# Keys of the first cross attention: when the sums are copied, where the heads' steps stand, which engine makes the low parts, and the order of the loads

## The chip, the core and the metric

The kernel runs on one core of one Trainium2 chip. The metric is the device time of one execution in microseconds, from before the first to after the last instruction. A core has five engines that take their instructions in the order written, each from its own queue, and wait for each other through semaphores: TensorE (PE, matmuls), VectorE (DVE), ScalarE (ACT), GpSimd (POOL) and SyncE (SP, which here only issues DMAs).

## The reference, cut to what matters

The whole is a decoder of two layers, each with a state-space block, a cross attention and a mixture of experts. The change touches the keys' half of the first cross attention, which has no softmax, so that keys and values can be multiplied first:

```python
# B = 4 batches, S = 1601 rows of context, D = 256, 16 heads of 64 (1024 columns)
c = layernorm(context) * ln1_g + ln1_b          # [B, 1601, 256]
K = l2norm_per_head(c @ wk)                     # [B, 1601, 16, 64]
V = c @ wv
attended = l2norm(Q) @ (K^T V) @ wo             # per head; K^T V = (K^T c) wv
```

The kernel computes G = c^T K (256 x 1024, summed over the 1601 rows of a batch), then for each pair of heads (128 columns) wv^T G, of which it keeps the two 64 x 64 blocks on the diagonal, and multiplies these with wo into P[b], which the queries' stage uses.

## The kernel before, in words

**Tiles.** 1601 rows are 13 tiles of up to 128 rows (`ST` = 13, the last has 65); with 4 batches there are 52 tiles, counted by i, tile t = i % 13 of batch b = i // 13. Every engine runs a loop over i, of two iterations more than tiles, and its instructions stand in the order in which the loop issues them.

**One iteration on each engine.**
- PE (`keys_pe`): `k_rows(i)`, 12 matmuls of 512 columns for the keys of tile i (each product is three, since both operands are split into a high and a low part; `mm3`, L109 to L111), then `turn(i + 1)` (L116, transposes the normalized context), one head step, `g_tile(i - 2)` (12 matmuls that add to the four banks of G; it waits for the high and low parts of keys and context), and one more head step.
- ACT (`keys_act`): copy of the keys from PSUM (L1100), high parts of the turned and the plain context of tile i+1 (L1070, L1073), square (L1109), high part of the normed keys of tile i-1 (L1080), square root of the sums (L1113), a step of `keys_normed_act` (the deviation of the context's rows, which waits for the statistics; in batch 3 `q_normed_act`), and two head steps.
- DVE (`keys_dve`): low parts of the context of tile i+1 (L952 from PSUM, L954 as the difference of two SBUF tiles), sum of squares (L984), low part of the keys of tile i-1 (`low`, L960), clamp, reciprocal, product with the keys in place (L988, L990, L993, "unit"), a step of `keys_normed_dve`, which normalizes the context of the next batch (three tiles of statistics, L882 and L886, or two tiles of affine steps, L897 and L900). Batch 0 has its own context normalized in three chunks beside the first tiles, and the next batch's behind them. At t = 12 what is left of it is run at once. In batch 3 the steps are `q_normed_dve`.
- POOL: two memsets. SP: all loads at the start, and stores of zeros to two DRAM buffers.

**The end of a batch.** In iteration i = 13 b + 14 PE runs the last `g_tile` of batch b. Behind it ACT copies half of G to `gT` (L1125) and DVE the other half (L1006), each at the end of its iteration. The head steps of the batch, 16 of them, are a generator (`keys_heads_pe`, `keys_heads_act`), two steps per iteration. Odd steps: PE multiplies `gT` with `wv` (L773, signal `hv`), ACT copies two blocks to `mT` (L1045, L1046, signal `hm`). Even steps: PE waits for `hm` and multiplies `mT` with `wo` (L780), ACT copies the product to `P` (L1050). The first step stands at the end of the iteration in which `gT` is copied, so an odd step always comes behind `g_tile` and an even one ahead of it. The heads and `turn` share two PSUM banks in the order of use (`Banks`).

**Memory.** `wk` is loaded into the buffer of `gT`; ACT casts its high part (L1083) and DVE subtracts (L964, 2048 columns).

Of the kernel before, what the change touches and what calls it, by code (L numbers as in the profile page):

```python
# [19 lines left out]
ST = 13  # L20
# [132 lines left out]
def step(g):  # L153
    next(g, None)
# [513 lines left out]
def keys_make(k, ctx, m):  # L668

    al = lambda shape, name, dt=F32: k.make(shape, dt, name=name, ctx=ctx)  # L670
    m.wk = [al([128, 2, 1024], "wk", F32R)[:, :, :] for _ in range(2)]
    m.wv = al([128, 2, 1024], "wv")
    m.wo = al([128, 8, D], "wo")

    m.cx = [k.gate.XF[:, 0:ST, :], al([128, ST, D], "cx")[:, :, :]]
    m.vnT = [[al([128, 2, 128], "vnT", F32R) for _ in range(2)] for _ in range(2)]
    m.cs = [[al([128, D], "cs", F32R) for _ in range(2)] for _ in range(4)]
    m.ks = [[al([128, 1024], "ks", F32R) for _ in range(2)] for _ in range(2)]
    m.cst, m.cmv = al([128, ST, 6], "cst"), al([128, ST, 2], "cmv")
    m.csd, m.crs = al([128, ST], "csd"), al([128, ST], "crs")  # L680
    m.gT = al([128, 2, 1024], "gT")
    m.mT = al([128, 8, 128], "mT")
    m.kv = k.psum[:, 4:6, :]
    m.tb = [k.psum[:, 6, :], k.psum[:, 7, :]]
    c = m.count
    tiles = B * ST
    m.w_v = c("wv_wo", 2, 16)
    m.w_k = c("wk", 1, 16)
    m.wk_hi, m.wk_lo = c("wk_high", 1), c("wk_low", 1)
    m.mt_zero = c("mT_zeroed", 1)  # L690
    m.ctx_in = [c(f"context{i}", 4, 16) for i in range(2)]
# [12 lines left out]


def xattn0_make(k, ctx, inner):
# [10 lines left out]
    c = m.count  # L717
    m.zeros = c("zeros", 1)
    m.w_q = c("wq", 1, 16)
    m.vecs = c("rows_of_all", 6, 16)  # L720
    m.q_mv, m.q_sd, m.q_rs = c("q_mean_var", B), c("q_dev", B), c("q_inv_dev", B)
    with ExitStack() as own:
        keys_make(k, own, m)
# [88 lines left out]
def keys_pe(k, m, pe):  # L812
# [43 lines left out]
    for i in range(n_tiles + 2):  # L856
# [16 lines left out]
def keys_normed_dve(k, m, dve, b, o):  # L873
# [1 line left out]
    g1, b1 = m.vec["ln1_g"], m.vec["ln1_b"]  # L875
    dve.memset(m.cmv[:, :, :], 1.0).then_inc(*k.v.up)
    filled = k.v.last()
    dve.wait_ge(*m.ctx_in[b % 2](2 * (b // 2) + 1))
    for n, (c0, c1) in enumerate(keys_chunks(b)):
        for t in range(c0, c1):  # L880
            q = ROWS[t]
            dve.bn_stats(m.cst[0:q, t, :], cx[0:q, t, :]).then_inc(*k.v.up)  # L882
# [54 lines left out]
def keys_dve(k, m, dve):  # L937
# [15 lines left out]
        dve.wait_ge(*m.ch(i))  # L953
        dve.tensor_tensor(cl[0:q, :], m.cx[b % 2][0:q, t, :], ch[0:q, :], ALU.subtract).then_inc(*m.cl.up)  # L954

    def low(i):
        w = ROWS[i % ST]
        kh, kl = m.ks[i % 2]
        dve.wait_ge(*m.kh(i))
        dve.tensor_tensor(kl[0:w, :], m.kn[i % 2][0:w, :], kh[0:w, :], ALU.subtract).then_inc(*m.kl.up)  # L960

    dve.wait_ge(*m.w_k(0))
    dve.wait_ge(*m.wk_hi(0))
    dve.tensor_tensor(m.wk[1], m.gT[:, :, :], m.wk[0], ALU.subtract).then_inc(*m.wk_lo.up)  # L964
    dve.wait_ge(*m.vecs(5))
    ahead = keys_normed_dve(k, m, dve, 0, seen[0])
    turned(0, ahead)
    first = ahead
    for i in range(n_tiles + 2):
        b, t = i // ST, i % ST  # L970
        if i < n_tiles:
# [6 lines left out]
                    pass  # L978
            if i + 1 < n_tiles:
                turned(i + 1, ahead)  # L980
            r = ROWS[t]
            kn, sq, rn = m.kn[i % 2], m.sq[i % 2], m.rn[i % 2]
            dve.wait_ge(*m.k_sq(i))
            dve.tensor_reduce(rn[0:r, :], sq[0:r, :].rearrange("p (h j) -> p h j", h=16), AX, ALU.add).then_inc(*m.k_sum.up)  # L984
            if i:
                low(i - 1)
            dve.wait_ge(*m.k_dev(i))
            dve.tensor_scalar(rn[0:r, :], rn[0:r, :], 1e-12, None, ALU.max).then_inc(*k.v.up)  # L988
            dve.wait_ge(*k.v.last())
# [2 lines left out]
            unit = kn[0:r, :].rearrange("p (h j) -> p h j", h=16)  # L992
            dve.tensor_tensor(unit, unit, rn[0:r, :].unsqueeze(2).to_broadcast([r, 16, 64]), ALU.mult).then_inc(*m.k_unit.up)  # L993
            step(ahead)
        elif i == n_tiles:
            low(i - 1)
        step(other)
        if i >= 2 and (i - 2) % ST == ST - 1:
            for _ in other:
                pass  # L1000
            other = keys_heads_order(own)
            pb = (i - 2) // ST
            dve.wait_ge(*m.g(i - 2))
# [50 lines left out]
def keys_act(k, m, act):  # L1054
# [20 lines left out]
    def high(i):  # L1075
# [12 lines left out]
    for i in range(n_tiles + 2):  # L1088
        b, t = i // ST, i % ST
        if i < n_tiles:  # L1090
# [18 lines left out]
            act.activation(sq[0:r, :], kn[0:r, :], ACT.Square).then_inc(*m.k_sq.up)  # L1109
            if i:  # L1110
                high(i - 1)
            act.wait_ge(*m.k_sum(i))
            act.activation(rn[0:r, :], rn[0:r, :], ACT.Sqrt).then_inc(*m.k_dev.up)  # L1113
            step(ahead)
        elif i == n_tiles:
            high(i - 1)
        step(other)
        if i >= 2 and (i - 2) % ST == ST - 1:
            pb = (i - 2) // ST
            for _ in other:  # L1120
                pass
            act.wait_ge(*m.g(i - 2))
            if pb:
                act.wait_ge(*m.hv(8 * pb - 1))
            act.copy(m.gT[:, 0, :].rearrange("p (a n) -> p a n", a=2), k.psum[:, 0:2, :]).then_inc(*m.g0.up)  # L1125
            other = keys_heads_act(k, m, act, pb, own)
        step(other)
    for _ in other:
        pass
# [2 lines left out]
def keys_sp(k, m, sp):  # L1132
    d = k.d

    def context(b):
        i = b % 2
        if b >= 2:

            sp.wait_ge(*m.cl(ST * (b - 1) - 1))
            sp.wait_ge(*m.vl(ST * (b - 1) - 1))  # L1140
        sp.dma_start(m.cx[i][:, 0:12, :], d["ctx"][b, 0:1536, :].rearrange("(t p) c -> p t c", p=128)).then_inc(*m.ctx_in[i].up)
        sp.dma_start(m.cx[i][0:ROWS[12], 12, :], d["ctx"][b, 1536:S, :]).then_inc(*m.ctx_in[i].up)

    sp.dma_start(m.wq[:, :, :], d["x0wq"]).then_inc(*m.w_q.up)
    for n in ("ln1_g", "ln1_b", "ln2_g", "ln2_b", "bo", "b2"):
        sp.dma_start(m.vec[n][:, :], row_of(k, "x0" + n, D)).then_inc(*m.vecs.up)
    sp.dma_start(m.wv[:, :, :], d["x0wv"]).then_inc(*m.w_v.up)
    sp.dma_start(m.wo[:, :, :], d["x0wo"]).then_inc(*m.w_v.up)
    sp.dma_start(m.gT[:, :, :], d["x0wk"]).then_inc(*m.w_k.up)
    context(0)  # L1150
    context(1)
    sp.wait_ge(*m.zeros(0))
    for j in range(TRASH // 256):
        sp.dma_start(k.DR["m0buf"][256 * j:256 * j + 256, :].rearrange("(t p) c -> p t c", p=128), k.zt[:, :, :]) \
# [2470 lines left out]
```

## Time and profile before

| | |
|---|---|
| time, median of 3 runs | 3018.78 us (3003.39 to 3024.97) |
| profiled execution | 3017.55 us, span 3015.7 us |
| PE busy | 2438.6 us, 81% of the span |
| DVE busy | 2197.7 us, 73% |
| ACT busy | 1444.9 us, 48% |
| POOL busy | 890.4 us, 30% |
| mean granted TensorE clock | 0.896 of full speed |

The profile is of one execution; its times are from the span's start. Busy shares are means over stages with different limits. The stage of the change lies between 552 and about 1003 us. "PEclk" is the granted clock as a share of full speed.

### The profile page before, as it was taken

How to read it: one execution, taken by the hardware profiler on the slowest of the kernel's cores; microseconds unless marked ns; L12 is line 12 of the kernel's file. 1: busy time of each engine (PE TensorE's matmuls, PEld its weight loads, DVE VectorE, ACT ScalarE, POOL GpSimd, SP SyncE). 2: the span in 40 equal slices, each digit the busy share in tenths (PEclk: the TensorE clock that was granted, in tenths of full speed). 3: DMA queues.
4: the chain of work that ended last, by engine and by line, in shares of the span. 5: the costliest groups of instructions: out<-in, count | busy, mean ns of one | idle time of the engine just before them, and what ended most of it. 6: DMA issues, size and time to landing. Idle time of an engine off the chain costs nothing.

```text
span 3015.7 us, 31540 instructions
## 1 busy us (share of the span) xinstructions
PE 2438.6 (81%) x10888; PEld 1591.5 (53%) x10888; DVE 2197.7 (73%) x3181; ACT 1444.9 (48%) x2547; POOL 890.4 (30%) x616
## 2 busy tenths in 40 slices
PE   4989886488888899948994598888667878799997
PEld 1333432266776565737883233343233434789997
DVE  5999999597886464326886699999955643567775
ACT  5656564245555222214563665656402435356673
POOL 2878776000000000020002377777601224100004
PEclk8999999798999799968996799999987876889999
DMA  4032030650000000022331302303056241246652
GB/s 165 2 112 99 14 113 0 242 172 1 23 1 1 33 1 1 1 103 95 106 120 42 135 24 89 112 1 113 0 130 133 48 88 51 90 144 219 222 183 84
DMA packets 100050, 249.56 MB, mean 83 GB/s; under 512 B 9410, under 2 KB 63567, under 8 KB 91944
## 3 DMA queue, kind: packets, MB, share of 16 engines
q1 hardware_dynamic: 83524, 222.64, 22.7%
q0 software_dynamic: 4608, 12.59, 1.3%
q10 hardware_dynamic: 11760, 12.32, 1.3%
q8 instruction: 87, 1.43, 0.2%
q14 instruction: 71, 0.58, 0.1%
HBM read 194.42 MB, written 53.10 MB: 82 GB/s over the span
## 4 chain that ended last, share of the span: by engine, by line
PE 46%; DVE 29%; ACT 11%; issue 9%; DMA 3%; POOL 1%; ACTq 1%; SPq 1%; another core or an unknown queue 0%; DVEq 0%; POOLq 0%
DVE psum L635 10%; PE psum L432 7%; PE psum L109 5%; PE psum L111 5%; PE psum L110 5%; PE psum L397 3%; PE psum L116 3%; DVE ch L643 3%; ACT g L3221 2%; PE psum L1238 2%; PE psum L1252 2%; ACT WH L3074 2%; PE psum L1222 2%; PE psum L1200 1%; PE psum L2523 1%
## 5 line engine op out<-in xcount | busy, mean ns | idle before, releaser
L317 POOL TENSOR_TENSOR bu<-u,row 128x1024 f32<-128x1024 f32 x254 | 597.8, 2358 | 286.7 <-DVE psum L635 190.3
L432 PE MATMUL psum<-ch,ident 128*128 128x512 f32 x1024 | 511.8, 629 | 139.6 <-DVE ch L643 139.1
L635 DVE TENSOR_TENSOR_SCAN psum<-psum,bu 128x1024 f32<-128x1024 f32 x256 | 585.4, 2287 | 18.7 <-ACT psum L514 18.5
L432 PEld LDWEIGHTS psum<-ch,ident 128*128 128x128 f32 x1024 | 188.3, 196 | 427.5 <-DVE ch L643 244.0
L514 ACT ACTIVATE psum<-dt,A 128x511 f32<-128x511 f32 x512 | 332.4, 682 | 0.4
L643 DVE TENSOR_TENSOR ch<-psum,row 128x1024 f32<-128x1024 f32 x256 | 313.0, 1223 | 7.6
L1508 POOL IOTA i<- 128x128 f32 x1 | 0.3, 346 | 758.5 <-DVEq L3366 758.5
L397 PE MATMUL psum<-hT,inw 128*128 128x512 f32 x256 | 138.8, 674 | 44.3 <-ACT sz L474 27.3
L3221 ACT ACTIVATE g<-psum,bias 128x256 f32<-128x256 f32 x248 | 101.0, 471 | 144.2 <-PE psum L111 132.3
L109 PE MATMUL psum<-WH,hs 128*128 128x256 f32 x496 | 145.7, 294 | 10.5 <-DVE hs L3301 7.1
L109 PE MATMUL psum<-xT,WH 128*128 128x256 f32 x496 | 141.2, 285 | 7.6 <-DVE xT L3264 7.6
L2651 DVE TENSOR_REDUCE mp<-psum 128x1 f32<-128x128 f32 (+1 forms) x192 | 85.7, 506 | 77.6 <-PE psum L2425 77.4
L111 PE MATMUL psum<-xT,WH 128*128 128x256 f32 x496 | 140.6, 284 | 1.1 <-issue 1.1
L110 PE MATMUL psum<-WH,hs 128*128 128x256 f32 x496 | 140.7, 284 | 0.3 <-issue 0.3
L110 PE MATMUL psum<-xT,WH 128*128 128x256 f32 x496 | 140.4, 283 | 0.6 <-DVE hs L3301 0.6
L111 PE MATMUL psum<-WH,hs 128*128 128x256 f32 x496 | 140.9, 284 | 0.0
L3301 DVE TENSOR_TENSOR hs<-g,hs 128x512 fp32r<-128x512 f32 x124 | 85.7, 692 | 73.2 <-ACT hs L3228 71.1
L2818 POOL TENSOR_SCALAR_AFFINE_SELECT pT<-pT 128x256 f32<-128x256 f32 x128 | 52.8, 414 | 265.1 <-ACT pT L2598 264.0
L3043 POOL DMA_INDIRECT R<-m1res,gi x26 | 26.7, 1025 | 344.7 <-DMA m1res<-ob 321.2
L2598 ACT ACTIVATE pT<-psum 128x1024 f32<-128x1024 f32 (+3 forms) x128 | 87.1, 706 | 85.1 <-PE psum L2508 84.2
L511 ACT COPY psum<-zero 128x2 f32<-128x2 f32 x256 | 41.2, 161 | 176.4 <-DVE ch L643 175.5
L3082 DVE TENSOR_TENSOR WH<-W,WH 128x1024 fp32r<-128x1024 f32 x96 | 113.1, 1220 | 7.9 <-ACT WH L3074 7.9
(403 smaller groups left out, 5915.1 us busy)
## 6 DMA issues: line engine op xcount, KB each, us to landing
W<-in_m1W SPq DMA_DIRECT2D x24, 2052.0 KB, 8.5
row<-Ascr SPq DMA_DIRECT2D x64, 512.0 KB, 4.8
row<-Bscr SPq DMA_DIRECT2D x64, 512.0 KB, 4.8
m1buf<-zt SPq DMA_DIRECT2D x8, 2048.0 KB, 16.8
W<-in_m0W SPq DMA_DIRECT2D x16, 1024.0 KB, 8.7
WH<-x1scr SPq DMA_DIRECT2D x16, 384.0 KB, 8.3
x1scr<-hi SPq DMA_DIRECT2D x48, 128.0 KB, 2.4
qk<-x1scr SPq DMA_DIRECT2D x16, 384.0 KB
```

What stands on the lines that cost most here:

```text
L109: pe.matmul(o, al, bh, start=start, stop=False)
L110: pe.matmul(o, ah, bl, start=False, stop=False)
L111: return pe.matmul(o, ah, bh, start=False, stop=stop)
L116: return pe.transpose(o, i, k.ident[0:n, 0:n])
L317: e.tensor_tensor(m.bu[i % 3][:, :, :], u, m.row[:, g, 0, :, :], ALU.mult).then_inc(*m.fed.up)
L397: p = pe.matmul(bank, m.inw[:, f, 128 * ob:128 * ob + 128], m.hT[:, f, :], start=f == 0, stop=f == 1)
L432: p = pe.matmul(m.y, k.ident, m.ch[i % RING_C][:, j, :], start=False, stop=g == UNITS - 1 and j == 1)
L514: e = act.activation(a[:, j, 1:T], m.dt[:, s % SIX, 1:T], ACT.Exp, scale=m.A[:, n:n + 1])
L635: dve.tensor_tensor_scan(flat, flat, m.bu[i % 3][:, :, :].rearrange("p a n -> p (a n)"), 0.0, ALU.mult, ALU.add).then_inc(*m.scan.up)
L643: dve.tensor_tensor(m.ch[i % RING_C][:, :, :], a, m.row[:, g, 1, :, :], ALU.mult).then_inc(*m.out.up)
L3082: dve.tensor_tensor(lo, w, hi, ALU.subtract).then_inc(*m.Wl.up)
L3221: e = act.activation(g[:, 256 * o:256 * o + 256], m.hb[j][:, 256 * o:256 * o + 256], ACT.Gelu_apprx_tanh, bias=m.bias[w % 3][:, 2 * j + o: ...
```

## The change

- `gT`: ACT and DVE copy G in iteration i = 13 b + 14 ahead of the square root and of the sum of squares of that iteration (`drawn`), no longer at its end.
- Heads: the new generator of head steps is made in the same iteration, but `continue` skips the step behind it, on PE, ACT and DVE. The first head step so comes in the next iteration, ahead of `g_tile`.
- Low parts of the keys and of `wk`: from DVE to POOL.
- Loads: `wk` first, then the first three tiles of context (a semaphore of their own), the two rows of the first layernorm, the rest of the context; `wq` and the other four rows come behind `wv`, `wo` and the second batch's context. DVE waits for the pieces where it uses them.

```diff
@@ -688,7 +688,7 @@
     m.w_k = c("wk", 1, 16)
     m.wk_hi, m.wk_lo = c("wk_high", 1), c("wk_low", 1)
     m.mt_zero = c("mT_zeroed", 1)
-    m.ctx_in = [c(f"context{i}", 4, 16) for i in range(2)]
+    m.ctx_first, m.ctx_in = c("context_first", 1, 16), [c(f"context{i}", 4, 16) for i in range(2)]
     m.c_mv, m.c_sd = c("context_mean_var", B + 2), c("context_dev", B + 2)
     m.c_n = c("context_normed", tiles)
     m.c_T = c("context_turned", tiles)
@@ -717,7 +717,7 @@
     c = m.count
     m.zeros = c("zeros", 1)
     m.w_q = c("wq", 1, 16)
-    m.vecs = c("rows_of_all", 6, 16)
+    m.vecs, m.ln_in = c("rows_of_all", 4, 16), c("first_ln_rows", 2, 16)
     m.q_mv, m.q_sd, m.q_rs = c("q_mean_var", B), c("q_dev", B), c("q_inv_dev", B)
     with ExitStack() as own:
         keys_make(k, own, m)
@@ -865,6 +865,7 @@
                 for _ in other:
                     pass
                 other = keys_heads_pe(k, m, pe, (i - 2) // ST, own)
+                continue
         step(other)
     for _ in other:
         pass
@@ -875,8 +876,11 @@
     g1, b1 = m.vec["ln1_g"], m.vec["ln1_b"]
     dve.memset(m.cmv[:, :, :], 1.0).then_inc(*k.v.up)
     filled = k.v.last()
-    dve.wait_ge(*m.ctx_in[b % 2](2 * (b // 2) + 1))
     for n, (c0, c1) in enumerate(keys_chunks(b)):
+        if b == 0 and n == 0:
+            dve.wait_ge(*m.ctx_first(0))
+        elif b or n == 1:
+            dve.wait_ge(*m.ctx_in[b % 2](2 * (b // 2) + 1))
         for t in range(c0, c1):
             q = ROWS[t]
             dve.bn_stats(m.cst[0:q, t, :], cx[0:q, t, :]).then_inc(*k.v.up)
@@ -890,6 +894,8 @@
                 yield
         yield
         dve.wait_ge(*m.c_sd(keys_chunk_at(b, n)))
+        if b == 0 and n == 0:
+            dve.wait_ge(*m.ln_in(1))
         dve.reciprocal(m.crs[:, c0:c1], m.csd[:, c0:c1]).then_inc(*k.v.up)
         for t in range(c0, c1):
             q = ROWS[t]
@@ -953,16 +959,15 @@
         dve.wait_ge(*m.ch(i))
         dve.tensor_tensor(cl[0:q, :], m.cx[b % 2][0:q, t, :], ch[0:q, :], ALU.subtract).then_inc(*m.cl.up)
 
-    def low(i):
-        w = ROWS[i % ST]
-        kh, kl = m.ks[i % 2]
-        dve.wait_ge(*m.kh(i))
-        dve.tensor_tensor(kl[0:w, :], m.kn[i % 2][0:w, :], kh[0:w, :], ALU.subtract).then_inc(*m.kl.up)
-
-    dve.wait_ge(*m.w_k(0))
-    dve.wait_ge(*m.wk_hi(0))
-    dve.tensor_tensor(m.wk[1], m.gT[:, :, :], m.wk[0], ALU.subtract).then_inc(*m.wk_lo.up)
-    dve.wait_ge(*m.vecs(5))
+    def drawn(i):
+
+        if i >= 0 and i % ST == ST - 1:
+            pb = i // ST
+            dve.wait_ge(*m.g(i))
+            if pb:
+                dve.wait_ge(*m.hv(8 * pb - 1))
+            dve.tensor_copy(m.gT[:, 1, :].rearrange("p (a n) -> p a n", a=2), k.psum[:, 2:4, :]).then_inc(*m.g1.up)
+
     ahead = keys_normed_dve(k, m, dve, 0, seen[0])
     turned(0, ahead)
     first = ahead
@@ -978,12 +983,11 @@
                     pass
             if i + 1 < n_tiles:
                 turned(i + 1, ahead)
+            drawn(i - 2)
             r = ROWS[t]
             kn, sq, rn = m.kn[i % 2], m.sq[i % 2], m.rn[i % 2]
             dve.wait_ge(*m.k_sq(i))
             dve.tensor_reduce(rn[0:r, :], sq[0:r, :].rearrange("p (h j) -> p h j", h=16), AX, ALU.add).then_inc(*m.k_sum.up)
-            if i:
-                low(i - 1)
             dve.wait_ge(*m.k_dev(i))
             dve.tensor_scalar(rn[0:r, :], rn[0:r, :], 1e-12, None, ALU.max).then_inc(*k.v.up)
             dve.wait_ge(*k.v.last())
@@ -992,19 +996,16 @@
             unit = kn[0:r, :].rearrange("p (h j) -> p h j", h=16)
             dve.tensor_tensor(unit, unit, rn[0:r, :].unsqueeze(2).to_broadcast([r, 16, 64]), ALU.mult).then_inc(*m.k_unit.up)
             step(ahead)
-        elif i == n_tiles:
-            low(i - 1)
+        else:
+            drawn(i - 2)
         step(other)
         if i >= 2 and (i - 2) % ST == ST - 1:
             for _ in other:
                 pass
             other = keys_heads_order(own)
-            pb = (i - 2) // ST
-            dve.wait_ge(*m.g(i - 2))
-            if pb:
-                dve.wait_ge(*m.hv(8 * pb - 1))
-            dve.tensor_copy(m.gT[:, 1, :].rearrange("p (a n) -> p a n", a=2), k.psum[:, 2:4, :]).then_inc(*m.g1.up)
+            continue
         step(other)
+    dve.wait_ge(*m.vecs(3))
 
 
 def both(a, b):
@@ -1078,6 +1079,14 @@
             act.wait_ge(*m.g(i - 2))
         act.wait_ge(*m.k_unit(i))
         act.copy(m.ks[i % 2][0][0:w, :], m.kn[i % 2][0:w, :]).then_inc(*m.kh.up)
+
+    def drawn(i):
+        if i >= 0 and i % ST == ST - 1:
+            pb = i // ST
+            act.wait_ge(*m.g(i))
+            if pb:
+                act.wait_ge(*m.hv(8 * pb - 1))
+            act.copy(m.gT[:, 0, :].rearrange("p (a n) -> p a n", a=2), k.psum[:, 0:2, :]).then_inc(*m.g0.up)
 
     act.wait_ge(*m.w_k(0))
     act.copy(m.wk[0], m.gT[:, :, :]).then_inc(*m.wk_hi.up)
@@ -1109,21 +1118,20 @@
             act.activation(sq[0:r, :], kn[0:r, :], ACT.Square).then_inc(*m.k_sq.up)
             if i:
                 high(i - 1)
+            drawn(i - 2)
             act.wait_ge(*m.k_sum(i))
             act.activation(rn[0:r, :], rn[0:r, :], ACT.Sqrt).then_inc(*m.k_dev.up)
             step(ahead)
-        elif i == n_tiles:
-            high(i - 1)
+        else:
+            if i == n_tiles:
+                high(i - 1)
+            drawn(i - 2)
         step(other)
         if i >= 2 and (i - 2) % ST == ST - 1:
-            pb = (i - 2) // ST
             for _ in other:
                 pass
-            act.wait_ge(*m.g(i - 2))
-            if pb:
-                act.wait_ge(*m.hv(8 * pb - 1))
-            act.copy(m.gT[:, 0, :].rearrange("p (a n) -> p a n", a=2), k.psum[:, 0:2, :]).then_inc(*m.g0.up)
-            other = keys_heads_act(k, m, act, pb, own)
+            other = keys_heads_act(k, m, act, (i - 2) // ST, own)
+            continue
         step(other)
     for _ in other:
         pass
@@ -1132,23 +1140,26 @@
 def keys_sp(k, m, sp):
     d = k.d
 
-    def context(b):
+    def context(b, t0=0):
         i = b % 2
         if b >= 2:
 
             sp.wait_ge(*m.cl(ST * (b - 1) - 1))
             sp.wait_ge(*m.vl(ST * (b - 1) - 1))
-        sp.dma_start(m.cx[i][:, 0:12, :], d["ctx"][b, 0:1536, :].rearrange("(t p) c -> p t c", p=128)).then_inc(*m.ctx_in[i].up)
+        sp.dma_start(m.cx[i][:, t0:12, :], d["ctx"][b, 128 * t0:1536, :].rearrange("(t p) c -> p t c", p=128)).then_inc(*m.ctx_in[i].up)
         sp.dma_start(m.cx[i][0:ROWS[12], 12, :], d["ctx"][b, 1536:S, :]).then_inc(*m.ctx_in[i].up)
 
-    sp.dma_start(m.wq[:, :, :], d["x0wq"]).then_inc(*m.w_q.up)
-    for n in ("ln1_g", "ln1_b", "ln2_g", "ln2_b", "bo", "b2"):
-        sp.dma_start(m.vec[n][:, :], row_of(k, "x0" + n, D)).then_inc(*m.vecs.up)
+    sp.dma_start(m.gT[:, :, :], d["x0wk"]).then_inc(*m.w_k.up)
+    sp.dma_start(m.cx[0][:, 0:3, :], d["ctx"][0, 0:384, :].rearrange("(t p) c -> p t c", p=128)).then_inc(*m.ctx_first.up)
+    for n in ("ln1_g", "ln1_b"):
+        sp.dma_start(m.vec[n][:, :], row_of(k, "x0" + n, D)).then_inc(*m.ln_in.up)
+    context(0, 3)
     sp.dma_start(m.wv[:, :, :], d["x0wv"]).then_inc(*m.w_v.up)
     sp.dma_start(m.wo[:, :, :], d["x0wo"]).then_inc(*m.w_v.up)
-    sp.dma_start(m.gT[:, :, :], d["x0wk"]).then_inc(*m.w_k.up)
-    context(0)
     context(1)
+    sp.dma_start(m.wq[:, :, :], d["x0wq"]).then_inc(*m.w_q.up)
+    for n in ("ln2_g", "ln2_b", "bo", "b2"):
+        sp.dma_start(m.vec[n][:, :], row_of(k, "x0" + n, D)).then_inc(*m.vecs.up)
     sp.wait_ge(*m.zeros(0))
     for j in range(TRASH // 256):
         sp.dma_start(k.DR["m0buf"][256 * j:256 * j + 256, :].rearrange("(t p) c -> p t c", p=128), k.zt[:, :, :]) \
@@ -1164,7 +1175,17 @@
 
 def keys_pool(k, m, pool):
     pool.memset(k.zt[:, :, :], 0.0).then_inc(*m.zeros.up)
+    pool.wait_ge(*m.w_k(0))
+    pool.wait_ge(*m.wk_hi(0))
+    pool.tensor_tensor(m.wk[1], m.gT[:, :, :], m.wk[0], ALU.subtract).then_inc(*m.wk_lo.up)
     pool.memset(m.mT[:, :, :], 0.0).then_inc(*m.mt_zero.up)
+    for i in range(B * ST):
+        w = ROWS[i % ST]
+        kh, kl = m.ks[i % 2]
+        if i >= 2:
+            pool.wait_ge(*m.g(i - 2))
+        pool.wait_ge(*m.kh(i))
+        pool.tensor_tensor(kl[0:w, :], m.kn[i % 2][0:w, :], kh[0:w, :], ALU.subtract).then_inc(*m.kl.up)
```

## Rows read from the trace of the kernel before

**Rows 1.** Windows: span, busy time and count of each engine, PEclk, DMA share, GB/s.

```profile
703.00:707.00 4.00, 4.00 (x12) 3.32 (x13) 0.00 (x0) 0.41 (x2) 0.00 (x0) 0.50 0.02 4
...
780.00:873.00 93.00, 84.41 (x391) 68.17 (x388) 78.93 (x147) 53.94 (x104) 0.00 (x0) 0.94 0.00 1
```

**Rows 2.** Timeline of one tile with heads: start us, us, engine, line, operation.

```profile
801.38 1.01 ACT L1100 COPY kn<-psum 128x1024 f32<-128x1024 f32 x1 [3.73 <-PE psum L111]
...
801.64 0.58 PE L109 MATMUL psum<-ks,cs 128*128 128x512 f32 x1
...
803.82 1.05 ACT L1080 CAST ks<-kn 128x1024 fp32r<-128x1024 f32 x1
...
803.96 1.22 DVE L984 TENSOR_REDUCE rn<-sq 128x16 f32<-128x1024 f32 x1 [0.51 <-ACT sq L1109]
...
804.59 0.60 PE L773 MATMUL psum<-gT,wv 128*128 128x128 f32 x4
804.95 0.48 PE L109 MATMUL psum<-wk,vnT 128*128 128x512 f32 x1
805.10 1.22 DVE L960 TENSOR_TENSOR ks<-kn,ks 128x1024 fp32r<-128x1024 f32 x1
805.22 0.21 ACT L1113 ACTIVATE rn<-rn 128x16 f32<-128x16 f32 x1 [0.35 <-DVE rn L984]
...
805.34 0.35 ACT L1050 COPY P<-psum 128x256 f32<-128x256 f32 x1
...
805.81 0.21 ACT L1046 COPY mT<-psum 64x64 f32<-64x64 f32 x1
...
806.72 1.23 DVE L993 TENSOR_TENSOR kn<-kn,rn 128x1024 f32<-128x1024 f32 x1
...
807.97 1.01 ACT L1100 COPY kn<-psum 128x1024 f32<-128x1024 f32 x1 [1.95 <-PE psum L111]
```

**Rows 3.** Timeline, from tile 14 to tile 23.

```profile
693.03 1.01 ACT L1100 COPY kn<-psum 128x1024 f32<-128x1024 f32 x1 [1.89 <-PE psum L111]
...
702.78 1.20 PE L773 MATMUL psum<-gT,wv 128*128 128x128 f32 x4 [6.81 <-DVE gT L1006]
...
708.66 1.01 ACT L1100 COPY kn<-psum 128x1024 f32<-128x1024 f32 x1 [4.23 <-PE psum L111]
...
762.58 1.02 ACT L1100 COPY kn<-psum 128x1024 f32<-128x1024 f32 x1 [1.83 <-PE psum L111]
```

**Rows 4.** Three lines of code: duration ns min/median/max, first and last start.

```profile
L317 POOL TENSOR_TENSOR bu<-u,row x254: 2335/2357/2384, 56.4 to 2181.4; 128x1024 f32<-128x1024 f32 x127
...
L150 DVE TENSOR_SCALAR xn<-X,xmv,rms x16: 389/402/2441, 11.1 to 324.7; 128x256 f32<-128x256 f32 x16
...
L2172 DVE TENSOR_TENSOR pick<-i,oo x8: 191/192/441, 2407.1 to 2598.0; 128x32 f32<-128x32 f32 x8
```

**Rows 5.** Timeline of the routing in the last stage, POOL and DVE.

```profile
2408.49 0.41 POOL L2818 TENSOR_SCALAR_AFFINE_SELECT pT<-pT 128x256 f32<-128x256 f32 x1 [4.91 <-ACT pT L2598]
2408.49 0.44 DVE L2172 TENSOR_TENSOR pick<-i,oo 128x32 f32<-128x32 f32 x1
```

**Rows 6.** DMA issues from 545 to 640 us: KB each, median us to landing.

```profile
wq<-in_x0wq SPq DMA_DIRECT2D x1, 1024.0 KB, 4.6
```

**Rows 7.** Timeline of the stage's start.

```profile
568.72 1.90 ACT L1083 CAST wk<-gT 128x2048 fp32r<-128x2048 f32 x1 [17.01 <-DMA gT<-in_x0wk]
...
575.70 0.48 DVE L897 SCALAR_TENSOR_TENSOR XF<-XF,cmv,bc 128x256 f32<-128x256 f32 x1
...
578.52 0.77 PE L109 MATMUL psum<-wk,vnT 128*128 128x512 f32 x1 [1.01 <-DVE vnT L952]
```

**Rows 8.** Timeline of batch 3, ACT.

```profile
900.59 1.01 ACT L1100 COPY kn<-psum 128x1024 f32<-128x1024 f32 x1 [1.97 <-PE psum L111]
...
908.79 0.30 ACT L1033 ACTIVATE sd<-mv,t 128x4 f32<-128x4 f32 x1 [4.14 <-DVE mv L927]
...
956.97 1.02 ACT L1100 COPY kn<-psum 128x1024 f32<-128x1024 f32 x1 [1.82 <-PE psum L111]
```

## The prediction

> **What bounds the kernel now.** I read the busy shares first (no engine is full over the whole kernel), then the windows of the key stage, 552 to 1003 us, and last its timeline tile by tile. In [rows 1] the batch from 780 to 873 us shows TensorE busy for 84.4 of 93 us with VectorE at 78.9: TensorE sets the pace and waits only in places. I measure a tile from one start of ACT's copy of the keys (L1100) to the next and call the start K; the i-th tile's is K(i). In a tile with a head step K moves by 6.59 us [rows 2], 801.38 to 807.97. TensorE has no hole in it: one head matmul pair, the 12 matmuls of `g_tile` from 801.64, the next pair at 804.59, the 12 of `k_rows` from 804.95, whose end starts the copy 3.02 us later. Less the two head pairs (0.26 from 801.38 to 801.64, 0.36 from 804.59 to 804.95) that is 5.97; each pair also breaks the stream of matmuls, and I take 5.75 for a tile without heads. So an operation taken off VectorE is worth something only where VectorE is late, above all in batch 0, where it normalizes two batches (VectorE is busy for 78.9 of 93 us in a batch in which it does one).
>
> The places where TensorE does wait are the start (first keys at 578.52 [rows 7]) and the change of batch: K(14) to K(15) takes 693.03 to 708.66, 15.6 us, with TensorE idle for 6.81 until VectorE has copied its half of the sums [rows 3]. Behind that idle the granted clock is 0.50, the 1.2 GHz level [rows 1]. From the head pair to the next copy then takes 5.88 us (702.78 to 708.66) where it takes 3.38 at the full clock (804.59 to 807.97), so an idle of several us costs about 2 us more; I take 2.0 for the part that the new order keeps.
>
> **The start.** `wq`, the first load, lands 4.6 us after its issue [rows 6]; `wk` in its place lands at 552.0 + 4.6 = 556.6. ACT's cast takes 1.9 [rows 7], to 558.6. The low part, 2048 columns, is now GpSimd's. A GpSimd TENSOR_TENSOR of 1024 columns takes 2.357 [rows 4], so 2048 take about 4.8, to 563.4. The first three context tiles (384 KB) land about 1.5 us behind `wk`, VectorE's statistics end near 560, and its affine steps (575.70 before) would start there, but they read two SBUF operands. They wait for GpSimd, as the next part shows, to 563.4. From that step to the first key matmul takes 2.8 (575.70 to 578.52): 566.2 instead of 578.5, **−12**. Without that wait it would be −15.
>
> **The port.** GpSimd and VectorE stand in each other's way in this trace: a VectorE TENSOR_TENSOR of 32 columns with two SBUF inputs takes 0.192 (median) and 0.441 when a GpSimd operation of 0.41 starts in the same moment [rows 4, 5]; a VectorE TENSOR_SCALAR of 0.402 takes up to 2.441, which is longer by 2.04 and so most of a GpSimd TENSOR_TENSOR [rows 4]. VectorE's operations with a PSUM input and one SBUF input show nothing of that. The Trainium skill, SBUF — State Buffer, section "SBUF: two separate sides", calls it an exclusive lock: whichever of the two starts first has the shared pair for its whole instruction. That is a rule against this change; by it the sum is the one that I give, and if it did not hold the sum would be that of the second rival.
>
> In a tile the low part of tile i−1 now starts at K+3.5 (the cast of 803.82 ends at 804.87 [rows 2]) and ends at K+5.9. VectorE's reduce (803.96) is over at K+3.7; its clamp of the norms and its product (`unit`, two SBUF inputs) come next. Before, the low part of 1.22 stood between them and `unit` ended at K+6.5 (806.72 + 1.14 to the next start). Now they wait for GpSimd to K+5.9, and `unit` starts 0.5 later and ends at K+7.5. So the 1.14 us taken off VectorE come back as a wait of 2.2, and VectorE is later by 1 us in a tile. Where nothing is queued behind `unit` this is hidden. For batch 0, where each tile has up to 1.9 us of normalization behind it (four affine steps of 0.48 [rows 7]), I walked the order: the second tile loses the 1.1 whole, the later ones lie between no loss (the short difference `cs` gets in ahead of GpSimd) and 0.9 each (it does not). That is −3 (a little of the gain stays) to +12 for the batch; I take **+5**, nearest to half of the tiles losing. At tile 12 VectorE drains the normalization of batch 1, 26 affine steps in a row, and GpSimd's low part now cuts in: **+2.4** (0 if it is starved instead, since that tile's `g_tile` is not due). The few other tiles without heads get 0.1 to 0.3 each: **+2**. The last low part is on the path to the last sums: 2.36 for 1.22, **+1**.
>
> **The copies of the sums and the order of the heads.** ACT and VectorE now copy at K(14)+3.0, where `g_tile` of the last tile ends, before the reduce of tile 14; TensorE meanwhile runs the keys of tile 15. K(14) to K(15) falls from 15.6 to 5.75. What is queued behind VectorE's wait is its reduce, so everything of tile 14 there is 1.6 later: `unit` ends at 7.5 and three statistics at 9.1 after K(14).
>
> What is late next is TensorE's wait for `hm`. Before, the first head step stood behind `g_tile` and the parity was: product with `wo` (L780) ahead of `g_tile`, product with `wv` (L773) behind it. ACT made `mT` at the end of the tile (805.81) and TensorE needed it only after the next keys. Now the first step stands ahead of `g_tile`. So L773 comes ahead and L780 behind `g_tile`, in the same tile, and L780 waits for the two copies to `mT`, which stand in ACT's queue behind its cast and its Sqrt. Queued behind that wait are the keys of the next tile. The Sqrt starts at K+3.84 (805.22), and with no copy to `P` ahead of them the two mT copies end at K+4.4 (5.34 to 5.81 now holds P and one of them, and each takes 0.22). L780 and its step to the next matmul take about 0.4, the keys 3.02: K+7.8. A head tile so takes 7.8 for 6.6, with TensorE idle for 1.2 from K+3.3.
>
> For tiles 14 to 23, before 762.58 − 693.03 = 69.6 [rows 3]:
> - K(14) to K(15): 5.75.
> - K(15) to K(16): VectorE's `turned(16)` is late (9.1 after K(14)), so is the reduce, and with it Sqrt and mT: 9.1 if `cs` gets in ahead of GpSimd, 12 if not, each plus up to 2 for the clock after an idle of over 2 us. I take 12.
> - Tile 17: ACT's heads wait behind its wait for the statistics `c_mv`. The like of it in batch 3 starts at 908.79, 8.2 after 900.59 [rows 8]: `unit` ends at K+6.5, so the statistics of four tiles take 1.7 behind it. Here it is one tile's, about 0.6, so 7.1, plus 1.0 for the later `unit` = 8.1. Then 0.3 for ACT's step, 0.45 for mT, 0.4 for L780, 3.02 and 2.0 for the clock: 14.3.
> - Six more at 7.8: 46.8.
>
> The sum is 78.9, **+9.3**; twice (batches 1 and 2): **+18.6**.
>
> In batch 3 ACT waits for the statistics of the queries in tiles 42, 44 and 46. The wait ends at K+8.2 and now 1.0 later, at 9.2; ACT's step 0.2, mT 0.45, L780 0.4, keys 3.02 and 2.0 for the clock make 15.2 each. K(42) to K(49) was 956.97 − 900.59 = 56.4 [rows 8] and becomes 3 × 15.2 + 4 × 7.8 = 76.8, +20.4. K(40) to K(42) was 15.6 + 6.6 by the pattern of [rows 3]; now the copy of tile 41 waits behind ACT's wait for the query statistics (`g_tile` 3.0, VectorE's copy 1.2, reduce 1.1, Sqrt, clamp and port 1.0, `unit` 1.1, statistics 1.7, ACT 0.3: 9.4, taken as 9.5), and tile 41 takes 9.8 with a cold clock: 19.3, −2.9. Together **+17.5**.
>
> The loads moved back (`wq`, four rows) are wanted some 400 us later, and SP waits for nothing new ahead of them: 0. The added waits for `context_first` and `first_ln_rows` are in the start above.
>
> **Sum**: −12 + 5 + 2.4 + 18.6 + 17.5 + 2 + 1 = +34.5. The profiled execution took 3017.55 (span 3015.7), 1.2 under the median of 3018.78, so the same difference stands on the median: **3053**.
>
> **Rivals.**
> 1. *The heads cost nothing.* If mT were ready when `g_tile` ends and the port did not bite: start −15, batch 0 −6, three changes of batch at −9.8, rest 0: −50, 2969. For it: mT is short and ACT is busy for only 58% of a batch. Against: the Sqrt at K+3.84 waits for VectorE's reduce in every tile, and `g_tile` ends at K+3.3. Chance 0.08.
> 2. *The head order costs, the port does not.* Start −15, batch 0 −6, changes and head tiles +6, +6 and +12, tail +1: +4, 3023. The decider is whether `unit` and the affine steps wait for GpSimd; against it stands [rows 5], for it that the row is of a short operation. Chance 0.22.
> 3. *Slower still by the clock*: if each hole of 1.2 us in the 24 head tiles lets the granted clock fall as the long ones do, 24 × 2 = +48 on the forecast, 3100. It decides from the point where the holes make the clock fall; rows of before show none so short and regular. Chance 0.10.
> 4. *The early start does not come* (`wk` shares the DMA engines with the loads behind it and lands as late as before): the forecast without −12, 3065. Chance 0.08.
>
> The forecast itself has 0.52; its own bounds are −3/+12 for batch 0, 9.1/14 for tiles 15, 28 and 0 to 2.5 for each cold restart (eight of them): 3025 to 3073. The range leaves out rivals 1 and 3: 3015 to 3078. One per cent, 30 us, is about what this measurement can tell from no change; that bound is at 3049. Of the forecast's 0.52 I put 0.31 above it; with rivals 3 and 4 slower is 0.49. Rival 2 and the rest of the forecast: same 0.43. Faster 0.08.
>
> **What would show it.** In the changed profile: first key matmul near 566; VectorE's `unit` with durations above 1.23 or an idle ahead of it, while GpSimd's low part runs; TensorE idle about 1.2 us ahead of L780 in each head tile, released by ACT mT, and K to K 7.8; 15.6 us gone at the changes of batch; some 5 us of idle in tiles 17, 30, 42, 44, 46. Wrong would be: no idle ahead of L780 (rival 1), `unit` ending at K+5.8 (rival 2), a granted clock of 0.50 through the head tiles (rival 3).

## The result, and the profile after

The changed kernel took 3054.02 us (median of 4 runs, 3048.01 to 3057.87) where the kernel before took 3016.77 in the same comparison: a ratio of 1.0131, 95% interval 1.0107 to 1.0155. The prediction was 3053, with a range of 3015 to 3078.

The profiled execution took 3057.87 us (span 3055.4). The same view of one tile with heads as in [rows 2], now of the changed kernel (L1109 is the copy of the keys, L1081 the cast, L990 the reduce, L1188 the low part on POOL, L1123 the Sqrt, L992 the clamp, L1046 and L1047 the copies to `mT`, L997 `unit`):

```profile
751.62 1.02 ACT L1109 COPY kn<-psum 128x1024 f32<-128x1024 f32 x1 [2.36 <-PE psum L111]
751.64 0.61 PE L773 MATMUL psum<-gT,wv 128*128 128x128 f32 x4
...
754.07 1.05 ACT L1081 CAST ks<-kn 128x1024 fp32r<-128x1024 f32 x1
...
754.21 1.22 DVE L990 TENSOR_REDUCE rn<-sq 128x16 f32<-128x1024 f32 x1 [0.47 <-ACT sq L1118]
...
755.25 2.36 POOL L1188 TENSOR_TENSOR ks<-kn,ks 128x1024 fp32r<-128x1024 f32 x1 [5.60 <-ACT ks L1081]
755.47 0.22 ACT L1123 ACTIVATE rn<-rn 128x16 f32<-128x16 f32 x1 [0.35 <-DVE rn L990]
755.59 0.19 ACT L1046 COPY mT<-psum 64x64 f32<-64x64 f32 x1
755.71 1.93 DVE L992 TENSOR_SCALAR rn<-rn 128x16 f32<-128x16 f32 x1 [0.28 <-ACT rn L1123]
755.79 0.21 ACT L1047 COPY mT<-psum 64x64 f32<-64x64 f32 x1
...
756.14 0.67 PE L780 MATMUL psum<-wo,mT 128*128 128x256 f32 x2 [1.12 <-ACT mT L1047]
...
756.46 0.59 PE L109 MATMUL psum<-wk,vnT 128*128 128x512 f32 x1
...
757.97 1.23 DVE L997 TENSOR_TENSOR kn<-kn,rn 128x1024 f32<-128x1024 f32 x1
...
759.62 1.01 ACT L1109 COPY kn<-psum 128x1024 f32<-128x1024 f32 x1 [2.40 <-PE psum L111]
```

TensorE stands idle for 1.12 us ahead of L780, released by ACT's copy to `mT`, and a tile takes 8.00. The other thing to see is the clamp: 16 columns in 1.93 us, from its start until 757.64, just behind the end of POOL's instruction at 757.61. In the view of single lines, over all 52 tiles (min/median/max in ns, as in [rows 4]; the first row is the clamp of the kernel before, L988):

```profile
L988 DVE TENSOR_SCALAR rn<-rn x52: 161/168/175, 587.1 to 972.8; 128x16 f32<-128x16 f32 x48, 65x16 f32<-65x16 f32 x4
...
L992 DVE TENSOR_SCALAR rn<-rn x52: 172/1935/1973, 578.9 to 1018.7; 128x16 f32<-128x16 f32 x48, 65x16 f32<-65x16 f32 x4
...
L997 DVE TENSOR_TENSOR kn<-kn,rn x52: 1220/1224/1226, 579.4 to 1020.9; 128x1024 f32<-128x1024 f32 x48, 65x1024 f32<-65x1024 f32 x4
...
L960 DVE TENSOR_TENSOR cs<-XF,cs x26: 410/415/2625, 570.0 to 887.5; 128x256 fp32r<-128x256 f32 x24, 65x256 fp32r<-65x256 f32 x2
```

The change of batch, as in [rows 3] (L1089 and L969 are the early copies of the sums). The 15.6 us are gone, and the next tile is the late one, with 2.11 us of idle ahead of its L780:

```profile
696.63 1.01 ACT L1109 COPY kn<-psum 128x1024 f32<-128x1024 f32 x1 [2.04 <-POOL ks L1188]
...
700.00 1.02 ACT L1089 COPY gT<-psum 128x1024 f32<-128x1024 f32 x1
...
700.30 1.22 DVE L969 COPY gT<-psum 128x1024 f32<-128x1024 f32 x1
...
703.22 1.02 ACT L1109 COPY kn<-psum 128x1024 f32<-128x1024 f32 x1 [0.33 <-PE psum L111]
...
708.73 0.67 PE L780 MATMUL psum<-wo,mT 128*128 128x256 f32 x2 [2.11 <-ACT mT L1047]
...
713.78 1.01 ACT L1109 COPY kn<-psum 128x1024 f32<-128x1024 f32 x1 [3.98 <-PE psum L111]
```

Tile 42, as in [rows 8], with the wait for the queries' statistics (L1034) ahead of `mT`; below it the windows behind, at a granted clock of 0.50:

```profile
922.66 1.01 ACT L1109 COPY kn<-psum 128x1024 f32<-128x1024 f32 x1 [4.03 <-PE psum L111]
...
931.83 0.30 ACT L1034 ACTIVATE sd<-mv,t 128x4 f32<-128x4 f32 x1 [5.12 <-DVE mv L933]
...
932.58 1.19 PE L780 MATMUL psum<-wo,mT 128*128 128x256 f32 x2 [6.54 <-ACT mT L1047]
...
938.90 1.01 ACT L1109 COPY kn<-psum 128x1024 f32<-128x1024 f32 x1 [4.72 <-PE psum L111]
```

```profile
932.00:934.50 2.50, 1.92 (x5) 1.58 (x6) 0.18 (x1) 0.80 (x4) 0.00 (x0) 0.50 0.02 7
934.50:938.50 4.00, 4.00 (x11) 3.12 (x10) 0.00 (x0) 0.00 (x0) 0.00 (x0) 0.50 0.00 0
```

The start of the stage, as in [rows 7] (L1092 is the cast of `wk`, L1180 its low part on GpSimd, L903 the first affine step); its first load is now issued at 556.12 (552.00 before):

```profile
561.03 1.90 ACT L1092 CAST wk<-gT 128x2048 fp32r<-128x2048 f32 x1 [5.21 <-DMA gT<-in_x0wk]
...
563.08 4.54 POOL L1180 TENSOR_TENSOR wk<-gT,wk 128x2048 fp32r<-128x2048 f32 x1 [6.40 <-ACT wk L1092]
...
565.69 0.18 DVE L899 RECIPROCAL crs<-csd 128x3 f32<-128x3 f32 x1 [1.82 <-DMA bc<-in_bc]
565.90 2.00 DVE L903 SCALAR_TENSOR_TENSOR XF<-XF,cmv,bc 128x256 f32<-128x256 f32 x1
```

**The stage in parts.** The starts of all 52 copies of the keys, K(0) to K(51), were read from the timeline of ACT in each run (e1 to e8 are the experiments below); the stage runs from SP's first load in it to SP's first load in the next (1003.86 before). In us of one profiled execution each:

| part | before | after | e1 | e2 | e3 | e4 | e5 | e6 | e7 | e8 |
|---|---|---|---|---|---|---|---|---|---|---|
| first load to K(0) | 31.0 | 18.7 | 19.6 | 18.6 | 18.5 | 18.6 | 19.6 | 31.3 | 18.6 | 17.9 |
| K(0) to K(12) | 82.3 | 91.7 | 89.9 | 91.6 | 82.3 | 82.2 | 85.3 | 89.9 | 82.2 | 82.5 |
| K(12) to K(13) | 21.8 | 24.1 | 23.8 | 24.0 | 21.8 | 21.8 | 23.9 | 23.7 | 21.8 | 20.7 |
| K(14) to K(15) | 15.6 | 6.6 | 6.6 | 10.2 | 6.6 | 6.6 | 6.1 | 16.7 | 6.6 | 6.6 |
| K(14) to K(23) | 69.6 | 79.0 | 63.9 | 67.2 | 76.6 | 61.1 | 76.2 | 73.7 | 59.8 | 59.8 |
| K(27) to K(36) | 69.3 | 77.4 | 63.9 | 67.2 | 76.4 | 61.2 | 77.8 | 72.4 | 59.8 | 59.9 |
| K(40) to K(42) | 21.9 | 19.7 | 15.6 | 16.8 | 20.6 | 14.9 | 19.7 | 22.8 | 15.0 | 14.9 |
| K(42) to K(49) | 56.4 | 80.3 | 60.1 | 62.2 | 75.5 | 57.9 | 77.5 | 63.3 | 50.0 | 50.0 |
| stage | 451.9 | 495.9 | 441.4 | 455.8 | 470.0 | 418.2 | 483.7 | 482.8 | 407.2 | 405.2 |

The stage is 44.1 us longer, the medians differ by 37.3. The rest is the other stages, whose code the change leaves as it is: in these two profiles the stage starts 4.1 us later (556.12 for 552.00), and the part behind it took 2011.8 us before and 2003.4 after (span less end of stage). That part lies between 2002 and 2016 in the runs e1 to e4, so a difference of a few us in the whole time says nothing of this stage, and the stage's own parts are what to read.

### The profile page after: what moved, and what is told of

It reads as the page before. It is cut to its first block, busy times and chain, and to the rows that moved or that the text cites. A ratio compares the mean times of both kernels' runs of the same rounds, so it can differ in the third digit from the quotient of the medians.

```text
span 3055.4 us, 31592 instructions
## 1 busy us (share of the span) xinstructions
PE 2444.2 (80%) x10888; PEld 1589.1 (52%) x10888; DVE 2221.6 (73%) x3128; ACT 1445.8 (47%) x2547; POOL 1017.4 (33%) x669
## 4 chain that ended last, share of the span: by engine, by line
PE 41%; DVE 29%; ACT 13%; issue 9%; POOL 3%; DMA 3%; ACTq 1%; another core or an unknown queue 0%; SPq 0%; POOLq 0%; DVEq 0%
DVE psum L635 10%; PE psum L432 6%; PE psum L109 4%; PE psum L111 4%; PE psum L110 4%; PE psum L397 3%; PE psum L116 3%; DVE ch L643 3%; ACT WH L3095 2%; ACT g L3242 2%; PE psum L1259 2%; PE psum L1273 2%; DVE rn L990 2%; PE psum L1243 2%; PE psum L1221 1%
## 5 line engine op out<-in xcount | busy, mean ns | idle before, releaser
L635 DVE TENSOR_TENSOR_SCAN psum<-psum,bu 128x1024 f32<-128x1024 f32 x256 | 585.5, 2287 | 18.8 <-ACT psum L514 18.6
L1188 POOL TENSOR_TENSOR ks<-kn,ks 128x1024 fp32r<-128x1024 f32 (+1 forms) x52 | 124.1, 2387 | 333.1 <-ACT ks L1081 333.1
```

The costliest lines, as they stand in the source:

```text
L635: dve.tensor_tensor_scan(flat, flat, m.bu[i % 3][:, :, :].rearrange("p a n -> p (a n)"), 0.0, ALU.mult, ALU.add).then_inc(*m.scan.up)
L1188: pool.tensor_tensor(kl[0:w, :], m.kn[i % 2][0:w, :], kh[0:w, :], ALU.subtract).then_inc(*m.kl.up)
```

## The experiments

Runs e1 to e3 take out one suspect each, e4 two, e6 puts one part alone into the kernel before, e5 tests the port that VectorE and GpSimd share, e7 and e8 go on from e4. Each ratio is to the kernel before, timed in the same comparison: 3014.54 us for e1 to e4, 3006.76 for e5 to e8. Between these two groups compare ratios, not times. The code shown is in extracts; `...` marks what lies between.

**e1: the order of the heads.** On PE, ACT and VectorE, with an empty step ahead:

```diff
+def one_step_later(g):
+    yield
+    yield from g
...
-                other = keys_heads_pe(k, m, pe, (i - 2) // ST, own)
+                other = one_step_later(keys_heads_pe(k, m, pe, (i - 2) // ST, own))
```

> The changed kernel, but the head steps start one step later still, so that the product with wv stands behind the tile's matmuls for the sums and the product with wo ahead of them, as before the change. Theory A (TensorE's wait for mT in each head tile, behind the matmuls for the sums, costs 1.2 to 1.4 us a tile, and 6 to 7 more where ACT waits for statistics): head tiles fall from 7.98 to about 6.6, tile 17 from 13.9 to 9, tiles 42, 44, 46 from 16.1 to 10; two batches at -15, the last at -20: about -50, 3004 us, ratio to the kernel before 0.996. Theory B (the shared port is what makes the changed kernel slow, the order of the heads is harmless): no change, 3054, ratio 1.012.

Measured: 3004.99 us, ratio 0.9969 (0.9952 to 0.9987). The batches go from 79.0 to 63.9 and from 77.4 to 63.9, K(42) to K(49) from 80.3 to 60.1, the stage from 495.9 to 441.4. That is 54.5 us off the stage for the "about 50" of theory A, and 3005 for its 3004; theory B falls. A tile (L1114 is the copy of the keys) takes 6.6, TensorE has no idle ahead of L780, and L780 uses the `mT` of the tile before:

```profile
741.49 1.02 ACT L1114 COPY kn<-psum 128x1024 f32<-128x1024 f32 x1 [1.25 <-PE psum L111]
741.51 0.60 PE L780 MATMUL psum<-wo,mT 128*128 128x256 f32 x2
...
744.69 0.63 PE L773 MATMUL psum<-gT,wv 128*128 128x128 f32 x4
...
746.64 0.21 ACT L1052 COPY mT<-psum 64x64 f32<-64x64 f32 x1
...
748.11 1.01 ACT L1114 COPY kn<-psum 128x1024 f32<-128x1024 f32 x1 [1.26 <-PE psum L111]
```

**e2: the skipped step back**, the other way to the same order: the three `continue` (PE, VectorE, ACT) are taken out.

```diff
                 other = keys_heads_pe(k, m, pe, (i - 2) // ST, own)
-                continue
         step(other)
```

> The changed kernel without the skipped step: the first head step stands at the end of the tile in which the sums are copied, as before the change, with the copies still early. Theory A: head tiles as in the run before (6.6); TensorE now waits in tile 14 for the copies that follow the last sums, 1.2 us and its restart, so K(14) to K(15) about 7.8 for 6.6, and one tile with heads less at the end: about 3 us above the run before, 3007, ratio 0.997. Theory B: 3054 plus 4, ratio 1.013.

Measured: 3016.54 us, ratio 0.9999 (0.9981 to 1.0017). The direction is A's, the size isn't: K(14) to K(15) takes 10.2, not 7.8, and the stage is 14.4 longer than in e1, not 3. TensorE's wait for the copies is 2.22 us, 1.0 more than expected. Behind it the granted clock is 0.50 (703 to 705 us), and from L773 to the next copy of the keys takes 5.06 us (701.06 to 706.12) where [rows 2] has 3.38, 1.7 more. The two make up the 2.4 and a little over. Of the 14.4, batches 1 and 2 hold 6.6, batch 3 3.3, the part behind K(51) 3.4 and batch 0 1.8, less 1.0 at the start; in batch 0 the two kernels do the same, so even a part of the stage can differ by 2 us between two profiles. The run shows that skipping a step is worth having, if the order stays.

**e3: the low parts of the keys back on VectorE**, behind the reduce; `wk`'s stays on GpSimd.

```diff
...
             dve.tensor_reduce(...).then_inc(*m.k_sum.up)
+            if i:
+                low(i - 1)
             dve.wait_ge(*m.k_dev(i))
```

> The changed kernel with the low parts of the keys back on VectorE; the low part of wk stays on GpSimd and the heads' order is that of the change. Theory A with the port: the clamp falls from 1.94 to 0.17, batch 0's first 12 tiles from 91.7 to about 82, its drain from 24.1 to 21.8, tiles without heads from 6.1 to 5.75 (12 of them, -4), head tiles from 7.98 to 7.8 (-4), the tiles with statistics 1 us each (-5): about -25, 3029, ratio 1.004. Theory B: all of the loss is the port's, 2985 or less, ratio 0.99.

Measured: 3038.83 us, ratio 1.0079 (1.0053 to 1.0104); the stage falls by 25.9, as expected (25). The time was expected at 3029 and is 10 above it: the part behind the stage took 2012.1 us in this profile for 2003.4. Batch 0 is back at 82.3 and 21.8 to the tenth, tiles without heads are at 5.7. Head tiles were expected at 7.8 and stay at 7.99: the port has no part in them. Theory B (2985) falls.

**e4: e1 and e3 together.**

> The heads' order of the first run and the low parts of the keys on VectorE; early copies and loads as in the change. Theory A: the start keeps its 12 us, batch 0 as in the kernel before, each of three changes of batch 9 us shorter than there: 3017 - 12 - 27 = 2978, ratio 0.987. If both causes overlap (one hides the other), the sum of the two gains measured alone is larger than what both give together.

Measured: 2982.28 us for the 2978 expected, ratio 0.989 (0.9861 to 0.9919). The stage is 77.7 shorter than the changed one; e1 and e3 alone gave 54.5 and 25.9, 80.4 in all. The two causes hardly overlap, and they make up the whole loss: without them the change gains 33.7 us in the stage, 12.4 at the start, 8.4 and 8.1 in the batches with the first two changes, less at the third, where tile 41 waits for statistics.

**e5: which VectorE operations wait for GpSimd.** The kernel leaves out VectorE's clamp at 1e-12.

```diff
-            dve.tensor_scalar(rn[0:r, :], rn[0:r, :], 1e-12, None, ALU.max).then_inc(*k.v.up)
-            dve.wait_ge(*k.v.last())
             dve.reciprocal(rn[0:r, :], rn[0:r, :]).then_inc(*k.v.up)
```

> The changed kernel without VectorE's clamp of the norms at 1e-12 (left out: the maximum with 1e-12), so that the product with the norms, which reads two tensors in SBUF, is the first VectorE operation of the tile that can meet GpSimd's low part. Theory: every VectorE operation with two SBUF tensors as inputs waits for GpSimd's whole instruction, so the wait moves to the product: its median duration goes from 1.22 to about 2.7 us, and it still ends near K+7.1; head tiles stay 7.98, batch 0's 12 tiles fall from 91.7 by 3 us at most. Rival: only the clamp, a TENSOR_SCALAR, is held: the product stays at 1.22 us, ends at K+5.6, and batch 0 falls to about 80.

Measured (one run, 3038.69 us, so without an interval): the wait moves to `unit`, with a median of 2.700 us where 2.7 was expected; the rival's 1.22 is out. The reciprocal ahead of it, one input, is not held (0.25 us with POOL at work). Batch 0 falls by 6.4, more than the 3 expected: the reciprocal now runs beside GpSimd's instruction instead of behind it, and `unit` ends at K+7.07 (754.30 less 747.23) for K+7.58 in the changed kernel (759.20 less 751.62), which is 0.5 in a tile and about 6 in 12. The line of `unit` over all tiles, and one tile:

```profile
L995 DVE TENSOR_TENSOR kn<-kn,rn x52: 1220/2700/2747, 576.0 to 1003.3; 128x1024 f32<-128x1024 f32 x48, 65x1024 f32<-65x1024 f32 x4
```

```profile
750.86 2.36 POOL L1186 TENSOR_TENSOR ks<-kn,ks 128x1024 fp32r<-128x1024 f32 x1 [5.61 <-ACT ks L1079]
...
751.31 0.25 DVE L992 RECIPROCAL rn<-rn 128x16 f32<-128x16 f32 x1 [0.28 <-ACT rn L1121]
...
751.60 2.70 DVE L995 TENSOR_TENSOR kn<-kn,rn 128x1024 f32<-128x1024 f32 x1
```

**e6: one part alone, in the kernel before**: `low` is taken out of VectorE's queue and POOL gets the loop of the change.

> The kernel before with one part of the change alone: the low parts of the keys on GpSimd. Theory: the wait at the port and the longer low part cost what the run with the low parts back on VectorE gave: batch 0's 12 tiles 82.3 to about 92, its drain +2.3, tiles without heads 5.75 to 6.1 (12 of them, +4), the tile with the statistics c_mv +1 twice, the three with the queries' statistics +1 each, the end +1: +23, 3038, ratio 1.008. Rival: taking 1.1 us of each tile from VectorE helps where VectorE is late, batch 0 to 76, ratio 0.997.

Measured: 3028.29 us, ratio 1.0066 (1.0039 to 1.0094), which is +21.5 for the +23 expected; the stage is 30.9 longer in the profile. Slower, as the theory has it, batch 0 at 89.9; the rival's 76 is out.

**e7: e4, with ACT's head steps ahead of its wait for statistics.**

```diff
             act.activation(rn[0:r, :], rn[0:r, :], ACT.Sqrt).then_inc(*m.k_dev.up)
-            step(ahead)
...
-            continue
-        step(other)
+        else:
+            step(other)
+        if i < n_tiles:
+            step(ahead)
```

> The fourth run's kernel, with ACT's two head steps ahead of its step of the normalization, so that the copies to mT and P don't stand behind its wait for the statistics. ACT still can't copy the next keys before that wait ends at K+8.2, so tiles 42, 44, 46 take about 8.4 for 9.1 to 9.9 and the tiles behind them 6.7 for 7.9, tiles 17 and 30 about 7.3 for 8.2: stage 418 to 411, ratio to the kernel before 0.987 for 0.989. If the clock is what costs there and not the wait, no difference.

Measured: 2960.85 us, ratio 0.9848 (0.9821 to 0.9874), stage 407.2. A pair of tiles such as 44 and 45 takes 14.4 where e4 took 17.3, but not as expected: the tile with the wait stays at 9.1 and the one behind it falls to 5.3. In e4 the copies to `mT` stand right behind ACT's wait (it ends at 910.02, they start at 910.48); in e7 they stand ahead of it (898.29, the wait ends at 902.28). Why the tile behind then takes only 5.3 is open. The gain over e4 is measured in the stage (11 us, 418.2 to 407.2, in one profile of each); by the whole time it is not quite clear, since the intervals of the two ratios meet (0.9861 to 0.9919 and 0.9821 to 0.9874).

**e8: the low part of `wk` on VectorE too**, in its gap ahead of the first affine steps.

```diff
+    next(ahead)
+    dve.wait_ge(*m.w_k(0))
+    dve.wait_ge(*m.wk_hi(0))
+    dve.tensor_tensor(m.wk[1], m.gT[:, :, :], m.wk[0], ALU.subtract).then_inc(*m.wk_lo.up)
     turned(0, ahead)
```

> The seventh run's kernel with the low part of wk on VectorE too, between the statistics and the affine steps of the first tiles, where VectorE waits for the two rows of the layernorm. It takes 2.3 us there for GpSimd's 4.5, and no affine step waits for the port: first key matmul about 2 us earlier, K(0) at 16.6 us from the stage's first load for 18.6; ratio 0.986. If the start is set by the loads, no difference.

Measured: 2962.76 us, ratio 0.9839 (0.9799 to 0.988), not to be told from e7. K(0) comes 0.8 earlier, not 2. What is good in the change (early copies, order of the loads, a step skipped) is worth 1.1% by e4; ACT's new order of e7 is no part of the change, and with it and nothing left on GpSimd but memsets it is 1.6%.

## Why the prediction was right

The terms against the stage's parts in the table:

| term | predicted | measured |
|---|---|---|
| start | −12 | −12.3 |
| batch 0, 12 tiles | +5 | +9.4 |
| drain at tile 12 | +2.4 | +2.3 |
| K(14) to K(23), K(27) to K(36) | +9.3 each | +9.4, +8.1 |
| K(40) to K(49) | +17.5 | +21.7 |
| other tiles without heads | +2 | +4.0 |
| end | +1 | +1.6 |
| sum | +34.5 | +44.1 (medians +37.3) |

The measured terms are rounded one by one.

**The heads' order** was the step that carried the sum, and it is shown by e1: taking it away gives 54.5 us. Its size was 7.8 us for a head tile and is 7.98: L780 waits until K+4.5 as worked out, and the rest takes 3.48 (756.14 to 759.62) for 3.4. Tile 17 was put at 14.3 and takes 13.9, tile 15 at 12 and takes 10.6, since `cs` got its turn ahead of GpSimd there (L958 and L960 at 706.17 and 706.48, POOL at 706.85), the lower of the two bounds, with the slow clock on top. Tiles 42, 44, 46 were put at 15.2 and take 16.1: `mT` ended at K+9.8 for 9.9, but the restart costs 2.8 us (932.58 to 938.90 is 6.32, for the 3.48) where I took 2.0, though [rows 3] and [rows 2] give 2.5 (5.88 less 3.38).

**The port** was right in mechanism, shown by e3 and e5: VectorE waits for the end of GpSimd's instruction, and the 1.1 us taken off it return as a clamp that is 1.8 longer (1.935 for 0.168). Its term for batch 0 was mis-sized, 9.4 for 5. I gave the losing state (`cs` behind GpSimd) to half of the tiles; the trace has `cs` at 2.0 to 2.6 us in the last three of the twelve, and tiles 2 and 7, at the ends of the chunks, are 1.2 longer each. Which of the two starts first decides, in both directions:

```profile
609.88 0.42 DVE L960 TENSOR_TENSOR cs<-XF,cs 128x256 fp32r<-128x256 f32 x1
609.93 2.64 POOL L1188 TENSOR_TENSOR ks<-kn,ks 128x1024 fp32r<-128x1024 f32 x1 [3.72 <-ACT ks L1081]
...
655.05 2.40 POOL L1188 TENSOR_TENSOR ks<-kn,ks 128x1024 fp32r<-128x1024 f32 x1 [5.17 <-ACT ks L1081]
655.12 2.61 DVE L960 TENSOR_TENSOR cs<-XF,cs 128x256 fp32r<-128x256 f32 x1
```

With `cs` 0.05 us ahead it takes its 0.42 and GpSimd's instruction 2.64; with GpSimd 0.07 ahead, GpSimd takes 2.40 and `cs` 2.61. The Trainium skill, in SBUF — State Buffer, "SBUF: two separate sides", states that the first to start keeps the port for its whole instruction. This trace agrees: the late clamp ends with GpSimd's instruction (757.64 and 757.61), and the late `unit` of e5 ends 1.08 us behind it (754.30 and 753.22), which is nearly its whole own time of 1.22.

**A wait that I did not see**: the 11 tiles without heads behind batch 0 that stand outside the other terms are 4.0 us longer together, 0.36 each, most at 6.1 for about 5.75. ACT copies the keys of tile i into the buffer whose low part of tile i−2 GpSimd still reads. In [rows 2] the low part was over (805.10 + 1.22) 1.65 us before that copy started; now its end releases the copy, and TensorE's matmuls for the sums as well, 0.21 us late:

```profile
794.46 0.50 PE L109 MATMUL psum<-ks,cs 128*128 128x512 f32 x1 [0.21 <-POOL ks L1188]
...
794.50 1.01 ACT L1109 COPY kn<-psum 128x1024 f32<-128x1024 f32 x1 [2.06 <-POOL ks L1188]
```

**The start** came out by its total, with a path that differs: the load of `wk` landed 4.9 us after its issue and GpSimd took 4.54, but VectorE was held until 565.69 by the two layernorm rows as well. So the port cost 1.5 us there (the affine step at 565.90 took 2.00 for 0.48), not 3, and e8 won back 0.8.

**What was luck.** 3053 for 3054.02 is closer than the terms were. In the stage they are 9.6 us too low together, most of it in batch 0 (+4.4) and behind K(40) (+4.2). Outside the stage, for which nothing was forecast, the changed kernel's profile is 4.1 us longer ahead of it and 8.5 shorter behind it; no run shows a reason for either. So the spans differ by 39.7 us and the medians by 37.3. Errors offset inside a term too: in tiles 14 to 23, K(14) to K(15) took 6.59 for 5.75 (TensorE waits 0.58 us for VectorE's `vnT`, L958), tile 15 10.6 for 12, tile 17 13.9 for 14.3 and each of six head tiles 7.98 for 7.8, and the sum is 79.0 for 78.9.

**The rivals.** Rival 1 is out by the idle ahead of L780 and by e1, rival 2 by e3 and e5, rival 4 by the start. Rival 3 is out too: the granted clock between 690 and 800 us is 0.97, and between 743 and 760, where head tiles follow each other, it is 1.00, so the holes of 1.1 us do not lower it.

## What to carry to other kernels

When steps of a generator are dealt out to fixed slots, skipping one slot turns over which step stands ahead of the long work and which behind: look at which of them waits for another engine in the same round, because that wait now has everything behind it. Ask of each operation moved to GpSimd not only how long it takes but which VectorE operations with two SBUF tensors, or SBUF TENSOR_SCALARs, fall into its span: in these traces one that starts behind it does not end before it does. Measure the parts alone: here two losses of 54 and 26 us stood over a gain of 34.

## What the runs showed of the hardware that I had not expected

A VectorE TENSOR_SCALAR of only 16 columns, in place in SBUF, is held for what is left of GpSimd's instruction: 1.935 us (median of 52) for 0.168 in the kernel before. The reciprocal of the same 16 columns (0.25 us in e5, beside GpSimd), the reduce of 1024 (1.21 in the seven tiles in which GpSimd had started first) and the statistics (0.39) are not. And the order of arrival decides by less than a tenth of a us: `cs` takes 0.415 us in most tiles and 2.0 to 2.6 in three of 52, and the two cases shown above differ by 0.12 us in when it starts against GpSimd.
